# A vision tower on one core: constants and the first attention group loaded one stage ahead, attention output kept in 192 rows with its sums inverted early, row numbers copied by another engine

## The chip, the cores and the metric

The kernel runs on one core of a Trainium2 chip. A core has TensorE (PE, matrix multiplication into PSUM), VectorE (DVE), ScalarE (ACT), GpSimd (POOL) and SyncE (SP, which here only issues DMAs), one instruction stream each. They meet through semaphores. DMAs are issued by SP, ACT and POOL and carried by the core's 16 DMA engines. The metric is the device time of one launch in microseconds (us).

## The reference

The reference takes 8 images through a tower of two blocks, with 1030 tokens of 192 features per image:

```python
h = _L0_tok_ref(x, W0, b0, W1, b1, W2, b2)                 # patches of 8, 16, 32 pixels
h = concatenate([cls_tok, h], axis=1)
h = h + _L0_attn_ref(_layernorm(h), W_qkv, b_qkv)           # retention with a decay mask
h = h + _L0_ffn_ref(_layernorm(h), ...)                     # 16 experts pick their tokens, and a shared one
h = h + _L1_attn_ref(_layernorm(h), Wq, Wkv, Wo_ctx, ...)   # attention, below
h = h + _L1_ffn_ref(_layernorm(h), w_router, ...)           # 8 experts, 2 per token, and a shared one
```

The second block's attention has 12 heads of 16 features. The last 32 tokens ("latent") look at all 1030, the 998 before them only at each other, and each kind has its own output projection:

```python
kv = _heads(x @ Wkv);  q = _rope(q) * DH ** (-0.5);  kv = _rope(kv)
lkv = _ln(kv, ln_g, ln_b)
attn_lat = softmax(einsum('bid,bkd->bik', q_lat, kv))
attn_ctx = softmax(einsum('bid,bkd->bik', q_ctx, kv_ctx))
out_lat = _merge(attn_lat @ lkv) @ Wo_lat + bo_lat
out_ctx = _merge(attn_ctx @ lkv_ctx) @ Wo_ctx + bo_ctx
```

All is float32.

## The kernel before, in words

The work is a row of stages, each with its own block of instructions for every engine and a barrier at its end: patches, retention, route (with the first block's shared expert), experts, heads, attend, project, dispatch, mixture, output. Inside a block the order on each engine is the order of the code, written by hand with ring buffers and semaphore counts; there is no planner for it but in attend, where a written table gives the places of the latent steps. What a stage leaves for the next lies in DRAM (`h_rows`, `y_rows`, `qk_parts`, `o_parts`, `x_rows`), with a few exceptions.

*Constants.* Each stage has its own buffers for its constants and for an identity matrix `ident`. They are loaded at the start of the stage on SP's queue (in project on ACT's), and the stage's TensorE and DVE streams begin with a wait for all of them. In retention seven constants (L286) stand ahead of the first rows h_in (L289).

*heads* makes q, k and v of one image after another. For image b SP stores four parts of q and k (L1347, each waits for its part) and the values (L1350, L1352). The stage ends when the last image's stores have landed.

*attend* works on 24 groups of 4 heads, three to an image. A group needs 18 loads of q and k (L1697 to L1701) and two of v (L1705, L1707), in three buffers in turn. TensorE makes scores (L1772 for the maxima, L1846 for the exponentials), DVE reduces maxima (L1947), ACT takes exponentials (L1902), and TensorE multiplies by v (L1832). v has padding columns so that a head takes 32 rows of the result O [128 x 1030]: 16 features, one row with the sum of the exponentials, 15 unused. ACT copies O out of PSUM in two halves (L1892) when the group before is stored, DVE adds the latent columns (L1970), and POOL stores O with one DMA into `o_parts` (L1752).

*project* first loads all sums [96 x 1030] out of `o_parts`, inverts them on DVE (L2244) and stores them to `recips`. Then for each image SP loads op [128 x 3 x 1030] (L2082), the reciprocals spread over the rows (L2086, four DMAs) and the residual h_in (L2089). DVE scales (L2222), TensorE multiplies by Wo in 3 blocks of 128 rows for each of 9 token tiles and 2 kinds of job, 54 instructions to an image (L2140), DVE adds the residual (L2232) and takes the layer norm (L1242 to L1253), TensorE transposes (L2154) and makes the router's logits (L2162), and ACT stores.

*mixture* runs 72 chunks of 256 rows in a ring of 4. For each chunk POOL copies the row numbers to `idx` (L2693), runs a small addition `pad` (L2687), and gathers rows with two indirect DMAs (L2701); then it copies the numbers to `to` (L2707), again `pad`, and scatters the results with two indirect DMAs that add (L2715). Gathers are issued four chunks ahead. TensorE transposes the rows (L2745), makes the down projection of the chunk before (L2788) and gate and up of this one (L2763 to L2769). DVE multiplies the hidden values (hT), copies xT, and scales the results.

## Time and profile before

| | us |
|---|---|
| median of 3 runs (lowest, highest) | 4608.73 (4606.34, 4609.55) |
| the profiled execution's own time | 4602.88 |
| its span in the trace | 4601.2 |
| TensorE busy | 3963.6 (86%) |
| DVE busy | 2468.1 (54%) |
| ACT busy | 1440.2 (31%) |
| POOL busy | 1193.5 (26%) |
| mean granted clock of TensorE | 0.926 |

The first instructions behind each barrier stand at these times of the trace: retention 126.21, route 474.19, experts 890.55, heads 1807.85, attend 2124.69, project 3399.90, dispatch 3643.59, mixture 3975.27. POOL's set-up memsets are over at 131.8 in retention, 477.4 in route and 891.0 in experts. Busy shares are means over stages with different limits, so a stage's window and its timeline say more than these totals. POOL's busy time doesn't count the gaps in which it only issues.

### The profile page before, as it was taken

To read this page: it belongs to the slowest core of one execution; us is meant where nothing else is said; L and a number is where in the kernel's file an instruction comes from.
4 is the path that set the end of the run, shared out by engine and by line. 5 is a ranking of instruction groups with operands and counts; after the bars stand their busy time and mean duration, and the time that the engine had idled before them with its cause. 6 is when DMAs were issued, how large, how long until landed. Compare 5 with 4: busy or idle time off the path is not lost. (4 is left out here: it accounts for less than half of the span.)

```text
span 4601.2 us, 74362 instructions
## 1 busy us (share of the span) xinstructions
PE 3963.6 (86%) x24044; PEld 2468.0 (54%) x24046; DVE 2468.1 (54%) x4416; ACT 1440.2 (31%) x2890; POOL 1193.5 (26%) x1370
## 2 busy tenths in 40 slices
PE   8799787699999997665999999999958599898885
PEld 8688555466666665341333333333327466666664
DVE  1476368622222232886777777777714454444442
ACT  0122110011111111341777777777741111111110
POOL 0222000134444443553000000000013200277775
PEclk9899899899999998775999999999977699999998
DMA  6121111223222222345333233324139311377676
GB/s 211 48 66 52 38 41 35 66 51 66 63 59 59 59 60 62 111 138 107 51 63 48 48 61 57 47 48 66 34 91 249 92 32 52 93 163 160 157 161 149
DMA packets 335641, 381.02 MB, mean 83 GB/s; under 512 B 44708, under 2 KB 292035, under 8 KB 333823
## 3 DMA queue, kind: packets, MB, share of 16 engines
q1 hardware_dynamic: 255903, 289.44, 26.0%
q0 software_dynamic: 57856, 69.18, 8.9%
q10 hardware_dynamic: 21728, 20.14, 1.5%
q8 instruction: 122, 2.00, 0.2%
q14 instruction: 32, 0.26, 0.0%
HBM read 261.02 MB, written 123.33 MB: 84 GB/s over the span
## 5 line engine op out<-in xcount | busy, mean ns | idle before, releaser
L1947 DVE TENSOR_REDUCE at_mx<-psum 128x1 f32<-128x998 f32 (+1 forms) x768 | 886.6, 1193 | 261.2 <-PE psum L1772 260.8
L1902 ACT ACTIVATE at_p<-psum 128x512 f32<-128x512 f32 (+3 forms) x1536 | 851.7, 588 | 297.1 <-PE psum L1846 267.6
L1846 PE MATMUL psum<-at_q,at_k 99*128 99x512 bf16 (+3 forms) x1536 | 521.0, 382 | 20.9 <-issue 15.8
L1772 PE MATMUL psum<-at_k,at_q 96*128 96x512 bf16 (+3 forms) x1536 | 474.8, 392 | 67.0 <-DMA at_k<-qk_parts 29.6
L1832 PE MATMUL psum<-at_p,at_v 128*32 128x486 f32 (+3 forms) x3072 | 406.0, 601 | 1.0 <-ACT at_p L1902 0.7
L1846 PEld LDWEIGHTS psum<-at_q,at_k 99*128 99x128 bf16 (+1 forms) x1536 | 155.3, 102 | 424.9 <-ACT at_p L1902 268.0
L1158 ACT ACTIVATE ex_silu<-psum 128x384 f32<-128x384 f32 (+1 forms) x288 | 131.8, 458 | 773.0 <-PE psum L1102 643.2
L1189 DVE TENSOR_TENSOR ex_hT<-ex_silu,psum 128x384 f32<-128x384 f32 (+1 forms) x288 | 147.6, 513 | 415.4 <-ACT ex_silu L1158 270.4
L1752 POOL DMA_DIRECT2D o_parts<-at_o x24 | 13.0, 541 | 1245.3 <-DVE at_mx L1947 999.8
L1124 PE MATMUL psum<-ex_wd,ex_hT 128*128 128x192 f32 (+1 forms) x1728 | 291.5, 327 | 0.0
L1772 PEld LDWEIGHTS psum<-at_k,at_q 96*128 96x128 bf16 (+1 forms) x1536 | 152.2, 105 | 229.3 <-DVE at_mx L1947 64.0
L1124 PEld LDWEIGHTS psum<-ex_wd,ex_hT 128*128 128x128 f32 (+1 forms) x1728 | 264.1, 179 | 15.9 <-issue 3.6
L2826 ACT ACTIVATE mx_silu<-psum 128x256 f32<-128x256 f32 x216 | 83.0, 384 | 517.1 <-PE psum L2768 466.9
L2715 POOL DMA_INDIRECT h_rows<-mx_ys,mx_to x144 | 229.6, 1595 | 58.6 <-issue 58.4
L1050 POOL DMA_INDIRECT y_rows<-ex_ys,ex_to x144 | 223.3, 1550 | 33.4 <-issue 33.4
L1097 PE MATMUL psum<-ex_xT,ex_wg 128*128 128x384 f32 (+1 forms) x576 | 230.7, 482 | 0.0
L2855 DVE TENSOR_TENSOR mx_hT<-mx_silu,psum 128x256 f32<-128x256 f32 x216 | 91.1, 422 | 257.2 <-ACT mx_silu L2826 203.6
L1098 PE MATMUL psum<-ex_xT,ex_wu 128*128 128x384 f32 (+1 forms) x576 | 214.0, 453 | 0.0
L1102 PE MATMUL psum<-ex_xT,ex_wr 64*128 64x384 f32 (+1 forms) x576 | 204.8, 475 | 0.0
L1103 PE MATMUL psum<-ex_xT,ex_wr 64*128 64x384 f32 (+1 forms) x576 | 204.8, 475 | 0.0
L2701 POOL DMA_INDIRECT mx_xs<-x_rows,mx_idx x144 | 145.3, 1009 | 53.9 <-issue 50.8
L2788 PE MATMUL psum<-mx_wd,mx_hT 128*128 128x192 f32 x864 | 154.1, 329 | 0.8 <-DVE mx_ys L2865 0.8
(360 smaller groups left out, 6733.4 us busy)
## 6 DMA issues: line engine op xcount, KB each, us to landing
mx_wd<-in_e_dT SPq DMA_DIRECT2D x72, 288.0 KB
qk_parts<-hd_parts SPq DMA_DIRECT2D x32, 579.4 KB, 3.8
at_k<-qk_parts SPq DMA_DIRECT2D x144, 128.8 KB
at_q<-qk_parts SPq DMA_DIRECT2D x144, 124.8 KB
tok_p<-in_x SPq DMA_DIRECT2D x12, 1176.0 KB
mx_wg<-in_e_gT SPq DMA_DIRECT2D x72, 192.0 KB
mx_wu<-in_e_uT SPq DMA_DIRECT2D x72, 192.0 KB
o_parts<-at_o POOLq DMA_DIRECT2D x24, 515.0 KB
```

The lines of the kernel that those rows point to most:

```text
L1050: pool.indirect_dma_start(y, bass.IndirectOffsetOnAxis(ap=to[0:n, half, t:t + 1], axis=0), ys[0:n, half, t, :], None, compute_op=ALU.add). ...
L1097: g = pe.matmul(gate, wg[:, half, cols], xT[:, 0, toks], start=first, stop=not first)
L1098: u = pe.matmul(lift, wu[:, half, cols], xT[:, 0, toks], start=first, stop=not first)
L1102: g = pe.matmul(gate, wr[0:64, half, cols], xT[0:64, 1, toks], start=first, stop=not first)
L1103: u = pe.matmul(lift, wr[64:128, half, cols], xT[64:128, 1, toks], start=first, stop=not first)
L1124: mm = pe.matmul(psum[0:n, 4 + p % 2, (t % 2) * D:(t % 2 + 1) * D], hT[:, f, 128 * t:128 * t + n], wd[:, half, f, :], start=(f == 0), stop ...
L1772: mm = pe.matmul(psum[0:ctx_rows[t], 3 + 2 * ((PRO + n) % 2) + k, 0:w], Q[v][0:R6, j * 1024 + 128 * t:j * 1024 + 128 * t + ctx_rows[t]], K ...
L1832: mm = pe.matmul(psum[32 * j:32 * j + HV, 7, 0:w], V[u][0:n, t, j * HV:(j + 1) * HV], P[0:n, c % 2, j, 0:w], start=(t == 0), stop=(t == CT ...
L1846: pe.matmul(psum[0:n, i % RING, 0:w], K[u][:, j, 128 * t:128 * t + n], Q[u][:, j * 1024 + at:j * 1024 + at + w], start=True, stop=True).th ...
L1902: act.activation(P[0:n, c % 2, j, 0:w], psum[0:n, i % RING, 0:w], ACT.Exp).then_inc(exp_ready, 1)
L1947: dve.tensor_reduce(mx[0:ctx_rows[t], j * CT + t:j * CT + t + 1], pair(n)[0:ctx_rows[t], 0:CTX], AX_X, ALU.max).then_inc(s_free, 1)
L2715: pool.indirect_dma_start(y, bass.IndirectOffsetOnAxis(ap=to[:, r, t:t + 1], axis=0), ys[:, r, t, :], None, compute_op=ALU.add).then_inc(a ...
```

## The change

1. *Constants one stage ahead.* One `ident` is loaded in patches and kept. Retention's constants are loaded in patches (SP, behind the loads of the first two pairs), route's in retention (behind h_in), heads' in experts (behind the first two experts' weights), project's in attend (SP, behind the third group's loads), dispatch's in project (13 DMAs on ACT's queue at the start of the stage).
2. *Attend's first group* is loaded at the end of heads, on SP, ahead of the last image's stores.
3. *Attend's output* goes into `o_rows` [8 x 192 x 1030] without the unused rows: for each group four DMAs of 16 rows and four that bring a row of sums into a small buffer. DVE inverts them in the next group, and POOL stores them.
4. *project* no longer inverts sums. It loads 128 + 64 features per image, with 17 DMAs, and multiplies in two blocks instead of three, 36 instructions. ACT issues no constants of project.
5. *mixture*: the copies of the row numbers go from POOL to DVE.

The core of the diff:

```diff
-            for b in range(B - 3, B):
+            for b in range(B - 3, B - 1):
                 store(b)
+
+            for q in range(QC):
+                sp.wait_ge(parts_out[q], 16 * (B - 1))
+            load_quad(sp, qk_parts, 0, 0, first[0], first[1], loaded)
+            sp.wait_ge(v_stored, 32 * (B - 1))
+            load_quad_values(sp, v_rows, 0, 0, first[2], v_loaded)
+            store(B - 1)
...
-            load(0, 0)
             load(0, 1)
-            load_values(0, 0)
             load_values(0, 1)
             put_maxima(0, S_FREE0 + CT * QH + 3)
             load(0, 2)
             load_values(0, 2)
+            load_project_consts(sp, inp, project, project_in)
...
+            def store_shares(g):
+
+                pool.wait_ge(shares_ready, g + 2)
+                dst = recips[bass.ds(g, 1)].rearrange("a h (r c) -> (a h r) c", c=T)
+                pool.dma_start(dst, shares[:]).then_inc(shares_stored, 16)
+
+            def store(b, u, g, jobs, first=False):
                 pool.wait_ge(s_free, jobs)
                 pool.wait_ge(o_ready, 2 * g + 2)
-                dst = o_parts[bass.ds(b, 1), u].rearrange("b p n -> (b p) n")
-                pool.dma_start(dst, O[:]).then_inc(o_stored, 16)
+                pool.wait_ge(shares_ready, g + 1)
+                for j in range(QH):
+                    head = (u * QH + j) * DH
+                    dst = o_rows[bass.ds(b, 1), head:head + DH].rearrange("b d n -> (b d) n")
+                    pool.dma_start(dst, O[32 * j:32 * j + DH, :]).then_inc(o_stored, 16)
+                    row = O[32 * j + DH:32 * j + DH + 1, :].rearrange("a (r c) -> a r c", c=T)
+                    pool.dma_start(sums[NC * j:NC * (j + 1), :], row).then_inc(o_stored, 16)
+                if not first:
+                    store_shares(g - 1)
...
                 if h == 0:
-                    act.wait_ge(o_stored, g * 16)
+                    act.wait_ge(o_stored, g * STORE)
...
+            def shares_of(g):
+
+                dve.wait_ge(o_stored, g * STORE)
+                if not isinstance(g, int) or g:
+                    dve.wait_ge(shares_stored, (g - 1) * 16)
+                dve.reciprocal(shares[:], sums[:]).then_inc(shares_ready, 1)
...
                         dve.tensor_copy(O[:, CTX:SEQ], pair(n)[:, 0:LAT]).then_inc(s_free, 1)
+                        shares_of(g)
...
-            sp.dma_start(sums[:], o_parts.rearrange("b q (j r) n -> (b q j) r n", r=32)[:, DH, :]).then_inc(sums_in, 16)
-            sp.wait_ge(recip_ready, 1)
-            sp.dma_start(recips.rearrange("b h n -> (b h) n"), shares[:]).then_inc(recip_stored, 16)
-            sp.wait_ge(recip_stored, 16)
             sp.wait_ge(zeroed, ZEROED)
...
-                    sp.dma_start(op[:, half], o_parts[bass.ds(b, 1)].rearrange("a q p n -> p (a q) n")) \
-                        .then_inc(loaded[half], 16)
-                    for j in range(4):
-                        src = recips.rearrange("b (q j) n -> b j q n", j=4)[bass.ds(b, 1), j]
-                        sp.dma_start(recip[32 * j:32 * j + 32, half], src.broadcast_to([32, QUADS, SEQ])) \
-                            .then_inc(loaded[half], 16)
+                    src = o_rows[bass.ds(b, 1)].rearrange("a d n -> (a d) n")
+                    for f, (at, n) in enumerate(FEATS):
+                        sp.dma_start(op[0:n, half, f, :], src[at:at + n]).then_inc(loaded[half], 16)
+                    for h in range(HEADS):
+                        f, at = divmod(h * DH, 128)
+                        src = recips.rearrange("(b q) j n -> b (q j) n", b=B)[bass.ds(b, 1), h]
+                        sp.dma_start(recip[at:at + DH, half, f, :], src.broadcast_to([DH, SEQ])).then_inc(loaded[half], 16)
...
+            def rows_of(c, r, n_gathered):
+
+                if n_gathered is not None:
+                    dve.wait_ge(gathered[r], n_gathered)
+                here = ids[:, bass.ds(c * GS, GS)]
+                dve.tensor_tensor(idx[:, r, :], here, here, ALU.bitwise_or).then_inc(idx_ready, 1)
+
+            def rows_to(c, r):
+
+                if not isinstance(c, int) or c >= RING:
+                    dve.wait_ge(added, (c - RING + 1) * GATHER)
+                here = ids[:, bass.ds(c * GS, GS)]
+                dve.tensor_tensor(to[:, r, :], here, here, ALU.bitwise_or).then_inc(to_ready, 1)
...
                 hidden(c, i, r)
+                if ahead:
+                    rows_of(c + AHEAD, (r + AHEAD) % RING, None if first and r == 0 else (i + (r + AHEAD) // RING) * GATHER)
                 if following:
                     take_rows(c + 1, (r + 1) % RING, (i + (r + 1) // RING) * GATHER + GATHER)
+                rows_to(c, r)
```

Three places show what moves. The first is SP's queue at the end of heads and the start of attend. Before (hd_ is of heads, at_ of attend; `at_q0` is the first group's q):

```order
L1347 DMA qk_parts<-hd_parts 96x3x1030 x4
L1350 DMA v_rows<-hd_v_out 128x8x384
L1352 DMA v_rows<-hd_v_out 6x384
L1268 UNCONDITIONAL_BRANCH
L1687 UNCONDITIONAL_BRANCH
L1689 DMA at_ident<-in_ident 128x128
L1697 DMA at_q0<-qk_parts 16x4x998
```

After, with the end of the first group's loads:

```order
L1319 DMA at_k0<-qk_parts 16x4x1030
L1325 DMA at_v0<-v_rows 128x8x128
L1326 DMA at_v0<-v_rows 6x128
L1410 DMA qk_parts<-hd_parts 96x3x1030 x4
L1413 DMA v_rows<-hd_v_out 128x8x384
L1415 DMA v_rows<-hd_v_out 6x384
L1340 UNCONDITIONAL_BRANCH
L1769 UNCONDITIONAL_BRANCH
L1315 DMA at_q1<-qk_parts 16x4x998
```

The 20 loads of the first group have moved in front of the last image's stores, and the second group's loads now come first behind the branch into attend.

The second is POOL's stream in mixture, one chunk. Before:

```order
L2693 COPY mx_idx<-slot_rows 128x2
L2694 REGISTER_ALU
L2687 TENSOR_TENSOR mx_pad<-mx_ident 128x1
L2701 DMA mx_xs<-x3_rows,mx_idx 128x200 x2
L2707 COPY mx_to<-slot_rows 128x2
L2710 REGISTER_ALU
L2687 TENSOR_TENSOR mx_pad<-mx_ident 128x1
L2715 DMA h4_rows<-mx_ys,mx_to 8496x192 x2
```

After:

```order
L2765 TENSOR_TENSOR mx_pad<-ident 128x1
L2779 DMA mx_xs<-x3_rows,mx_idx 128x200 x2
L2785 REGISTER_ALU
L2787 REGISTER_ALU
L2792 REGISTER_ALU
L2765 TENSOR_TENSOR mx_pad<-ident 128x1
L2794 DMA h4_rows<-mx_ys,mx_to 8496x192 x2
```

Both copies are gone from POOL. The third is DVE's stream there, a chunk at the end of the stage. Before:

```order
L2855 TENSOR_TENSOR mx_hT<-mx_silu,psum 128x256 x3
L2834 TENSOR_TENSOR mx_hot_share<-mx_xs,chunk_hot 128x16
L2838 TENSOR_REDUCE mx_share<-mx_hot_share 128x2
L2843 COPY mx_xT<-psum 128x256
L2845 COPY mx_xT<-psum 64x256
L2846 COPY mx_xT<-psum 64x256
L2865 TENSOR_TENSOR mx_ys<-psum,mx_share 128x384
```

After:

```order
L2948 TENSOR_TENSOR mx_hT<-mx_silu,psum 128x256 x3
L2914 TENSOR_TENSOR mx_idx<-slot_rows 128x2
L2927 TENSOR_TENSOR mx_hot_share<-mx_xs,chunk_hot 128x16
L2931 TENSOR_REDUCE mx_share<-mx_hot_share 128x2
L2936 COPY mx_xT<-psum 128x256
L2938 COPY mx_xT<-psum 64x256
L2939 COPY mx_xT<-psum 64x256
L2921 TENSOR_TENSOR mx_to<-slot_rows 128x2
L2958 TENSOR_TENSOR mx_ys<-psum,mx_share 128x384
```

`mx_idx` is written between the hidden values and the copies of xT, `mx_to` between those copies and the results.

## Rows read from the trace of the kernel before

**Rows 1.** Windows, one per stage: busy us of each engine, clock, DMA share, GB/s.
```profile
890.00:1808.00 918.00, 884.31 (x4320) 603.58 (x4320) 260.91 (x528) 131.76 (x288) 392.30 (x450) 0.98 0.29 60
...
2125.00:3400.00 1275.00, 1188.74 (x9048) 399.26 (x9048) 947.92 (x984) 903.24 (x1705) 23.77 (x33) 0.96 0.32 51
3400.00:3643.00 243.00, 167.51 (x876) 150.89 (x876) 103.11 (x316) 36.24 (x88) 68.13 (x32) 0.70 0.73 188
...
3975.00:4569.00 594.00, 519.53 (x2880) 395.53 (x2880) 243.96 (x648) 82.98 (x216) 429.80 (x576) 0.98 0.70 156
```

**Rows 2.** Timeline, retention's start: SP's queue, DVE.
```profile
148.13 2.14 SPq L289 DMA_DIRECT2D ret_h_in<-h_rows  x4
...
154.17 1.14 DVE L507 BATCH_NORM_STATS2 ret_stats<-ret_h_in 103x6 f32<-103x192 f32 x4 [3.77 <-DMA ret_h_in<-h_rows]
```

**Rows 3.** Timeline, route's start: POOL, DVE.
```profile
476.83 0.52 POOL L683 MEMSET rt_zero<- 128x512 bf16 x1
...
486.22 0.77 DVE L829 COPY rt_gpad<-rt_gate 96x32 f32<-96x32 f32 x8 [11.83 <-DMA sh_wd<-in_sh_dT]
```

**Rows 4.** Timeline, heads' start: DVE, TensorE.
```profile
1821.09 2.67 DVE L1253 TENSOR_SCALAR hd_xn<-hd_rows,hd_mv,hd_rstd 128x192 f32<-128x192 f32 x9
...
1826.68 1.73 PE L1432 MATMUL psum<-hd_ident,hd_xn 128*96 128x128 f32 x7 [31.40 <-DMA hd_sin<-in_rope_sin]
```

**Rows 5.** Timeline, starts of experts (POOL) and dispatch (POOL, DVE).
```profile
892.44 0.19 POOL L1025 COPY ex_idx<-ids 128x9 int32<-128x9 int32 x1 [1.43 <-DMA ex_ident<-in_ident]
...
3645.13 0.57 POOL L2373 MEMSET di_slot<- 128x576 f32 x1
...
3655.22 0.23 DVE L2477 CAST di_iota_lo<-di_iotas 128x128 bf16<-128x128 f32 x1 [26.22 <-DMA di_wd<-in_s_dT]
```

**Rows 6.** Timeline and window, end of heads, start of attend: SP's queue, POOL, TensorE.
```profile
2104.70 10.29 SPq L1347 DMA_DIRECT2D qk_parts<-hd_parts  x4
...
2135.59 0.29 POOL L1746 CAST at_identb<-at_ident 128x128 bf16<-128x128 f32 x1
...
2140.70 1.82 PE L1772 MATMUL psum<-at_k,at_q 96*128 96x512 bf16 x4 [29.64 <-DMA at_k<-qk_parts]
...
2125.00:2150.00 25.00, 7.94 (x17) 1.26 (x18) 8.19 (x8) 0.00 (x0) 10.70 (x8) 0.50 1.04 121
```

**Rows 7.** Steady attend: timeline of POOL and ACT; dispatch's POOL DMAs by line.
```profile
3308.13 0.53 POOL L1752 DMA_DIRECT2D o_parts<-at_o  x1 [48.55 <-DVE at_mx L1947]
...
3330.91 0.58 ACT L1892 COPY at_o<-psum 128x512 f32<-128x512 f32 x1
...
L2381 POOL DMA_DIRECT2D x_rows<-di_expd x9: 601/886/1431, 3674.0 to 3681.6; - x9
```

**Rows 8.** Timeline, end of attend and start of project: POOL, DVE.
```profile
3393.64 0.53 POOL L1752 DMA_DIRECT2D o_parts<-at_o  x1 [38.71 <-ACT at_o L1892]
...
3403.42 6.59 DVE L2244 RECIPROCAL pr_shares<-pr_sums 96x1030 f32<-96x1030 f32 x1 [26.64 <-DMA pr_sums<-o_parts]
...
3436.68 3.38 DVE L2222 TENSOR_TENSOR pr_on<-pr_op,pr_recip 128x3090 f32<-128x3090 f32 x1 [1.72 <-DMA pr_hin<-y_rows]
```

**Rows 9.** Project's scalings by line, and two windows of the stage.
```profile
L2222 DVE TENSOR_TENSOR pr_on<-pr_op,pr_recip x8: 3351/3356/3379, 3436.7 to 3595.3; 128x3090 f32<-128x3090 f32 x8
...
3436.00:3455.00 19.00, 11.74 (x54) 10.94 (x54) 6.21 (x10) 0.00 (x0) 7.11 (x2) 0.75 1.06 262
...
3579.00:3596.00 17.00, 16.19 (x81) 15.10 (x80) 13.16 (x43) 2.42 (x6) 7.05 (x2) 0.71 0.35 102
```

**Rows 10.** Mixture: POOL's copies by line; timeline of POOL and TensorE.
```profile
L2693 POOL COPY mx_idx<-slot_rows x13: 751/761/771, 4198.4 to 4294.6; 128x2 int32 x13
...
4199.43 0.19 POOL L2687 TENSOR_TENSOR mx_pad<-mx_ident 128x1 f32<-128x1 f32 x1 [0.23 <-POOL mx_idx L2693]
...
4198.26 0.65 PE L2745 MATMUL psum<-mx_ident,mx_xs 128*128 128x128 f32 x4 [1.88 <-DMA mx_xs<-x_rows,mx_idx]
...
4205.28 0.66 PE L2745 MATMUL psum<-mx_ident,mx_xs 128*128 128x128 f32 x4
```

More of the change, by code:

```diff
@@ L2092, in _ @@
         def _(pool):
-            for buf in (wo[:], gain[:], shift[:], hin[:], mv[:], xn[:], logits):
+            for buf in (hin[:], mv[:], xn[:], logits):
                 pool.memset(buf, 0.0).then_inc(zeroed, 1)
@@ new lines, in build @@
+        project = project_consts(ctx, nc)
+        with ExitStack() as quads:
+            first = quad_buffers(quads, nc, 0)
+            with ExitStack() as middle:
+                heads = heads_consts(middle, nc)
+                phase_experts(nc, psum, inp, xg, y, ids, ident, ident_in, heads, heads_in)
+                phase_heads(nc, psum, inp, y, qk_parts, v_rows, ident, ident_in, heads, heads_in, first, loaded, v_loaded)
+            phase_attend(nc, psum, inp, qk_parts, v_rows, o_rows, recips, ident, ident_in, first, loaded, v_loaded,
+                         project, project_in)
@@ new lines, in build @@
+        slots = sb("slot_rows", [128, NSL], I32)[:]
+        chunk_expert, chunk_hot = sb("chunk_expert", [1, NCH], I32)[:], sb("chunk_hot", [128, NCH, E1])[:]
+        with ExitStack() as late:
+            dispatch = dispatch_consts(late, nc)
+            x3T = late.enter_context(nc.sbuf_tensor("x3T", [DP, DC, B, SEQ], F32))[:]
+            logits = late.enter_context(nc.sbuf_tensor("logits", [128, NTC * B, E1], F32))[:]
+            phase_project(nc, psum, inp, o_rows, recips, y, h3, x3T, logits, xg3, ident, ident_in, project, project_in,
+                          dispatch, dispatch_in)
+            phase_dispatch(nc, psum, inp, h3, x3T, logits, h4, xg3, slots, chunk_expert, chunk_hot, ident, ident_in,
+                           dispatch, dispatch_in)
@@ L2920, in build @@
+        phase_mixture(nc, psum, inp, xg3, h4, slots, chunk_expert, chunk_hot, ident, ident_in)
         phase_output(nc, h4, out)
```

428 lines of the change are left out of this document (219 added, 209 removed).

## The prediction

> **What bounds the kernel now.** I read the table of windows first, since the stages have different limits [rows 1]. In attend TensorE is busy 1188.7 of 1275 us at a clock of 0.96: that stage is TensorE's, and only its ends can be won. In project TensorE is busy 167.5 of 243 us at 0.70, DVE 103.1, and the DMA engines 0.73: three partners hand on to each other. In mixture TensorE is busy 519.5 and POOL 429.8 of 594 us; POOL's figure leaves out issue gaps, so the timeline has to decide there. Then I read the timeline of each stage's first microseconds [rows 2 to 5], because every stage ends in a barrier and whatever is loaded behind it stands on the path; then the boundary heads to attend [rows 6], one group of attend [rows 7], the start and period of project [rows 8, 9], and the loop of mixture [rows 10].
>
> **Constants, stage by stage.** *Retention* [rows 2]. The four h_in loads are issued at 148.13 because seven constants stand ahead of them on SP's queue; the first statistics follow at 154.17, 6.0 later. The barrier is over at 126.2 (the list of stage starts ahead), so after the change h_in is issued there and the statistics start at 132.3; POOL's memsets are over at 131.8 and don't hold them: −21.9. The constants, some 0.8 MB, go behind the patches' first two pairs' loads and wait for nobody there. *Route* [rows 3]. DVE waits until 486.22 for sh_wd; POOL's last memset ends at 477.4. −8.8. *Experts* [rows 5]. POOL's first copy waits for ident until 892.44, its memset was done at 891.0: −1.4. *Heads* [rows 4]. The xn of the first tile is written from 1821.09, TensorE starts at 1826.68, held by sin. With the constants there it starts about 1.3 behind 1821.09: −4.3. *Dispatch* [rows 5]. DVE waits until 3655.22 for di_wd. The logits are there and POOL's last memset ends at 3645.7, so DVE starts there: −9.4. *Mixture* starts like experts: −1.4. Together −47.2. Each stands on a row that names a constant's landing as the last releaser; what is late next is named above (memsets, h_in). Bounds −40 to −50. If the covers were gone (heads' 3.75 MB go beside experts, DMA share 0.29 [rows 1]), each would pay its own row again, at most.
>
> **Heads to attend.** SP's order changes (the first of the three places shown with the change). Before, SP stores the last image part by part from 2104.70, the stage ends at 2124.7, attend's first group is issued behind that, and TensorE starts at 2140.70 [rows 6]. After, 20 loads of the first group (about 1.5 MB of q and k, 0.5 MB of v) stand ahead of the last image's stores, and the 18 of q and k wait until the image before has landed. Attend's start: POOL's cast of identb, behind its memsets, ends at 2135.88, 11.2 behind the barrier, so TensorE can start at +11.5 rather than at +16: −4.5. Heads' end: 2 MB at the 121 GB/s of the row is 16 us, the queue is empty in part, and the four parts become ready one after another over 10.3 us (the length of the row at 2104.70), which covers part of it; I take +7.5 (bounds 0 and +12). Net +3, from −4.5 to +7.5. This is the one edit I expect to lose.
>
> **Attend.** One POOL DMA of 0.53 us per group becomes nine. In the steady state POOL stores O at 3308.13, and ACT writes it again at 3330.91 [rows 7]: 22.8 us. A POOL DMA cost 0.53 here and 0.89 in dispatch, so the eight are issued in 4.3 to 7.1 us, and with 3.3 to land they are done in 7.6 to 10.4. Hidden. DVE gets one reciprocal of 103 elements a row per group: by the 6.59 us for 1030 [rows 8] 0.7 us, on an engine busy 948 of 1275 us [rows 1]. For that I take +2, bounds 0 and +8. The Trainium skill (DMA: Bandwidth & Descriptors, section Anatomy of one DMA) speaks against the split: each DMA of this path costs some 2.0 us whatever its size, plus its bytes over 436 GB/s, and its section Bandwidth asks for 1 MiB per transfer. By that, eight one behind the other (66 KB and 4 KB in turn) would take an estimated 16.6 us, still inside the window, but 9 us more at the end of attend: a sum of −135 instead of −144. No row here shows eight in a row.
>
> **Project's start.** Before: the last POOL store at 3393.64, the reciprocal 96x1030 of 6.59 us at 3403.42, first scaling at 3436.68 [rows 8], 43.0 us from the store. After: eight POOL DMAs (+4.6), landing 3.3 (in either kernel a guess from the block's end 6.3 behind the store), the small reciprocal 0.8, the store of the shares with its landing 4.0: attend ends near 3406.5 instead of 3399.9. Then op, recip and hin of image 0, 2.4 MB, need 10 to 13 us at 180 to 260 GB/s and 15 issues some 8 us: scaled at 3424 to 3427. Dispatch's constants, 1.1 MB, now run on ACT's queue at the same moment: +3 (4 us at 262 GB/s, part of it beside POOL's memsets). So 3429.7 instead of 3436.7: −7 (bounds −13 and 0).
>
> **Project's period.** The eight scalings run from 3436.7 to 3595.3, 22.7 us apart [rows 9]. The DMA engines are at 1.06 in the first of them and at 0.35 in the last stretch, so they bound the stage most of the time, not always. Bytes per image: op and recip 2 x 1.58 MB, hin 0.79, two stores of 0.79: 5.5 MB. After: 2 x 0.79 + 0.79 + 1.58 = 3.95 MB, 0.71 of it: 16.2 us. TensorE's work of one image is 81 instructions of 16.2 us at a clock of 0.71 (the last stretch); 18 of its 54 products of 0.22 go: 12.3, and with the hand-overs some 14.8. DVE loses 2 x 128x1030 in part, 3.36 us to about 2.2. I take 16.5, above both: 7 x 6.2 = −43, and −3 for the last image: −46. Bounds: −20 (SP needs 17 issues per image instead of 8, and waits on stores stay) and −60.
>
> **Mixture.** POOL's copies start 8.01 us apart (13 starts, 4198.4 to 4294.6), and POOL waits for nothing but itself [rows 10]. The order shows two COPY rows less per chunk. The copy in front of the gather overlaps the DMA ahead of it but for some 0.2, and the pad behind it waits 0.23 for it (the row at 4199.43); the copy in front of the scatter, 0.2 long, the same: 0.86 together, POOL's round goes to 7.15. TensorE waits 1.88 us for the gather at 4198.26, and its one unblocked round is 4198.26 to 4205.28, 7.02. Into its chain goes rows_of, which DVE now does between hT and the copies of xT that TensorE needs: about 0.2, so 7.2. Two rounds so close collide now and then: I take 7.3. (8.01 − 7.3) x 69 = −49. Bounds: −59 (7.15) and −15 (7.8, if rows_of and rows_to both add their wait, some 0.3 each, to TensorE's chain and the gather comes later by it).
>
> **Sum.** −47.2 +3 +2 −7 −46 −49 = −144. The profiled execution's own time was 4602.9 (span 4601.2, 1.7 around it); that gives 4459. It lay 5.9 under the median of the runs shown, 4608.7, so I forecast 4464.5.
>
> **Rivals.**
> (1) *Mixture keeps its time.* DVE's rows become the bound: TensorE's chain 7.02 + 0.6 and the hand-over give 7.8. For: no slack was seen between DVE's last copy of xT and TensorE. Against: DVE is busy 244 of 594 us. Time 4464.5 + 34 = 4498.
> (2) *Project isn't bound by bytes.* The small DMAs, 17 per image, take SP's queue 12 us and more, and the store to load waits stay: 20 us per image, −20. For: the share falls to 0.35 at the end without a shorter period. Time 4464.5 + 26 = 4490. With (1), 4524.
> (3) *The boundaries cost more*: heads ends 12 later instead of 7.5 and attend's first groups are late, or POOL's eight DMAs at the end of attend go one behind the other: in series, each with the 3.3 until it has landed, they take 26 us; for the end alone +9 to +18: 4474 to 4483.
> (4) *More than forecast*: mixture at 7.15, project at 15: 4464.5 − 10 − 14 = 4440.
> (5) *Slower.* Attend's DMAs don't fit the window: ACT's copy at 3330.91 stalls, and behind it the exponentials that TensorE waits for. It costs from (22.8 − 3.3)/8 = 2.4 us per DMA on, and 23 groups pay. For no gain they would need 6.3 us more per group, 3.2 us per DMA; for slower by 0.2% 3.3 us and above: 4618 and more. Against: 0.53 and 0.89 in the rows, 1.43 the longest. In series at 3.3 each the eight would overrun the window by 3.6 us, 23 times: +83, 4547, still faster.
> (6) *The change doesn't do what it says*: constants hidden before already. The releasers in rows 2 to 5 exclude it for the constants; if project and mixture both gave nothing, 4560.
>
> **How the numbers follow.** Chances: forecast (4448 to 4480) 0.46, (1) 0.15, (2) 0.13, both 0.05, (3) 0.06, (4) 0.08, (5) 0.03, (6) 0.04. What a measurement tells from no change is 0.2%, about 9 us. Slower is (5), 0.03, and same a partial (5) or (6), 0.02: faster 0.95. The range takes in (1) to (4): from 4425 (both large terms at their favourable bound, −59 and −57) to 4520 (short of (1) and (2) together), and leaves 0.2 outside.
>
> **What would show it.** In the profile after: the first statistics of retention near 132; TensorE's start of attend 11.5 us behind its barrier, and heads longer by 7; in attend no wait of ACT for a DMA at the copy of O; scalings 16 to 17 us apart in project; POOL's pads ahead of the gather 7.2 to 7.4 apart in mixture, with no copy on POOL. I would be wrong by a lot if TensorE's clock changed: it stood at 0.70 in project, and at a lower share of the full clock its chain of 14.8 becomes the bound; or if DVE's waits for landed scatters, which it didn't have before, came on TensorE's path.

## The result and the profile after

The changed kernel takes 4569.3 us (median of 4 runs, 4568.0 to 4576.5), the kernel before 4609.1 on the same chip: ratio 0.9916 [0.9903, 0.9929]. That is 40 us faster where I forecast 144, and outside my range of 4425 to 4520. The profiled execution took 4569.56 us, its span 33.4 less than that of before.

The page of the kernel after: span, busy times, and the clock in 40 slices.

```profile
span 4567.8 us, 74772 instructions
...
PE 4034.8 (88%) x23898; PEld 2458.2 (54%) x23898; DVE 2484.5 (54%) x4593; ACT 1438.0 (31%) x2890; POOL 1249.9 (27%) x1415
...
PEclk9999988899999998775999999999975589999998
```

TensorE has fewer instructions in project than before, and yet 71 us more busy time over the whole kernel. In the second group of low digits of PEclk, three quarters of the way along, stand two fives: that is project. Split by stage, from POOL's first instruction behind each barrier to the next one's, and mixture from its first gather to its last scatter (us):

| | before | after | change | forecast |
|---|---|---|---|---|
| patches | 126.2 | 130.8 | +4.6 | 0 |
| retention | 348.0 | 328.4 | −19.6 | −21.9 |
| route | 416.4 | 415.7 | −0.7 | −8.8 |
| experts | 917.3 | 918.3 | +1.0 | −1.4 |
| heads | 316.8 | 323.9 | +7.1 | +3.2 |
| attend | 1275.2 | 1278.0 | +2.8 | +4.1 |
| project | 243.7 | 262.4 | +18.7 | −59.6 |
| dispatch, mixture's start | 334.1 | 324.0 | −10.1 | −10.8 |
| mixture's chunks | 591.1 | 553.8 | −37.3 | −49 |
| sum | 4568.8 | 4535.3 | −33.5 | −144.2 |

Project alone misses by 78 of the 111 us. Here are its windows after (columns as in [rows 1]), its TensorE timeline over one image, and the waits of DVE (us in total, times, longest).

```profile
3440.00:3480.00 40.00, 37.67 (x111) 23.69 (x112) 19.54 (x75) 6.06 (x13) 11.07 (x5) 0.50 0.58 167
3480.00:3520.00 40.00, 38.16 (x137) 23.74 (x137) 17.27 (x57) 6.91 (x17) 7.84 (x5) 0.59 0.49 131
```

```profile
3441.56 16.52 PE L2246 MATMUL psum<-pr_wo_g,pr_on 128*128 128x192 f32 x36 [2.81 <-DVE pr_on L2320]
3458.00 2.29 PE L2260 MATMUL psum<-ident,pr_xn 128*96 128x128 f32 x9
3460.61 2.22 PE L2260 MATMUL psum<-ident,pr_xn 128*96 128x128 f32 x9 [0.31 <-ACT pr_xT L2303]
3463.30 7.15 PE L2268 MATMUL psum<-pr_router,pr_xT 96*128 96x8 f32 x36 [0.47 <-ACT pr_xT L2303]
3470.37 4.76 PE L2246 MATMUL psum<-pr_wo_g,pr_on 128*128 128x192 f32 x10
```

```profile
DVE pr_hout L2331 <- PE psum L2246: 56.1, 26, 3.9
...
DVE pr_hout L2331 <- DMA h_rows<-pr_hout: 7.9, 4, 3.9
```

The 36 products of an image take 16.5 us; 54 took 10.5 to 12.0 before (11.74 in the first window of [rows 9], at a clock of 0.75). TensorE goes from one piece of work to the next with gaps of 0.3 to 0.5 us: busy 38 of 40 us, at 0.50, the lower of its two levels (1.2 of 2.4 GHz). The DMA share has gone down to 0.58 and 0.49. Nobody waits long for a store any more (7.9 us in all, where before DVE waited 31.1 and 27.7 us for the stores of `pr_hout` and `pr_xn`); DVE waits for TensorE. So the bytes did shrink as forecast, and TensorE became the bound with a period of 26 to 29 us (the first products of the images from the second on start at 3441.6, 3470.4, 3496.9, 3524.4, 3553.2, 3579.9 and 3606.4).

Mixture: TensorE's transposes of two chunks (timeline), POOL's pads, DVE's new row, and a window.

```profile
4204.84 0.66 PE L2824 MATMUL psum<-ident,mx_xs 128*128 128x128 f32 x4
...
4212.36 0.66 PE L2824 MATMUL psum<-ident,mx_xs 128*128 128x128 f32 x4
```

```profile
4212.14 0.75 POOL L2765 TENSOR_TENSOR mx_pad<-ident 128x1 f32<-128x1 f32 x1
...
4215.99 0.19 POOL L2765 TENSOR_TENSOR mx_pad<-ident 128x1 f32<-128x1 f32 x1 [0.65 <-DVE mx_ys L2958]
```

```profile
4205.70 0.15 DVE L2914 TENSOR_TENSOR mx_idx<-slot_rows 128x2 int32 x1
```

```profile
4200.00:4300.00 100.00, 97.99 (x538) 72.79 (x538) 47.57 (x147) 15.68 (x41) 75.25 (x81) 1.00 0.72 172
```

The same window of before had TensorE busy 90.4 us. Now it is busy 98 of 100, and POOL waits at times for DVE's results (0.65 us at 4215.99): the bound has passed from POOL to TensorE, at 7.5 us a round.

The starts of the stages, timeline rows after: SP and DVE in retention, DVE in route, TensorE in heads, DVE in dispatch.

```profile
130.75 1.85 SPq L319 DMA_DIRECT2D ret_h_in<-h_rows  x4
...
136.78 2.17 DVE L539 BATCH_NORM_STATS2 ret_stats<-ret_h_in 103x6 f32<-103x192 f32 x8 [0.20 <-DMA ret_h_in<-h_rows]
...
462.36 0.78 DVE L846 COPY rt_gpad<-rt_gate 96x32 f32<-96x32 f32 x8 [3.00 <-POOL rt_zero L699]
...
1807.59 2.32 PE L1502 MATMUL psum<-ident,hd_xn 128*96 128x128 f32 x9 [26.82 <-DVE hd_xn L1288]
...
3659.74 0.23 DVE L2557 CAST di_iota_lo<-di_iotas 128x128 bf16<-128x128 f32 x1 [17.34 <-POOL di_slot L2452]
```

No constant is a releaser any more: the engines wait for h_in, for POOL's memsets and for xn, as each row of [rows 2 to 5] was expected to end. In route DVE starts 3.2 us behind the barrier at 459.2 (before 12.0), and the stage still takes as long. A window of route after, with the clock in the third column from the end:

```profile
685.00:725.00 40.00, 31.31 (x339) 22.58 (x338) 31.91 (x25) 2.05 (x4) 0.00 (x0) 0.80 0.12 32
```

Its counterpart before, from 700:

```profile
700.00:740.00 40.00, 31.31 (x366) 22.35 (x358) 34.67 (x28) 3.08 (x6) 0.00 (x0) 0.94 0.13 33
```

The end of heads and start of attend, and steady attend (ACT's copy is the one that overwrites the O that POOL has stored):

```profile
2094.59 7.07 SPq L1410 DMA_DIRECT2D qk_parts<-hd_parts  x4
...
2128.26 0.29 POOL L1815 CAST at_identb<-ident 128x128 bf16<-128x128 f32 x1
...
2128.61 1.85 PE L1858 MATMUL psum<-at_k,at_q 96*128 96x512 bf16 x4 [31.92 <-POOL at_identb L1815]
...
3292.60 0.50 POOL L1830 DMA_DIRECT2D o_rows<-at_o  x1 [44.19 <-DVE at_mx L2033]
...
3296.61 0.55 POOL L1821 DMA_DIRECT2D recips<-at_shares  x1
...
3315.39 0.58 ACT L1978 COPY at_o<-psum 128x512 f32<-128x512 f32 x1
```

And the end of attend, POOL and DVE:

```profile
3378.13 0.50 POOL L1830 DMA_DIRECT2D o_rows<-at_o  x1 [34.68 <-ACT at_o L1978]
...
3381.63 0.52 POOL L1832 DMA_DIRECT2D at_sums<-at_o  x1
...
3383.89 0.79 DVE L2053 RECIPROCAL at_shares<-at_sums 40x103 f32<-40x103 f32 x1 [21.92 <-DMA recips<-at_shares]
...
3384.97 0.52 POOL L1821 DMA_DIRECT2D recips<-at_shares  x1 [2.28 <-DVE at_shares L2053]
...
3395.11 2.98 POOL L2199 MEMSET pr_hin<- 128x3456 f32 x1 [9.62 <-POOLq L62]
```

### The profile page after: what moved, and what is told of

It reads as the page before. It is cut to its first block and busy times, and to the rows that moved or that the text cites. A ratio compares the mean times of both kernels' runs of the same rounds, so it can differ in the third digit from the quotient of the medians.

```text
span 4567.8 us, 74772 instructions
## 1 busy us (share of the span) xinstructions
PE 4034.8 (88%) x23898; PEld 2458.2 (54%) x23898; DVE 2484.5 (54%) x4593; ACT 1438.0 (31%) x2890; POOL 1249.9 (27%) x1415
## 5 line engine op out<-in xcount | busy, mean ns | idle before, releaser
L1932 PE MATMUL psum<-at_q,at_k 99*128 99x512 bf16 (+3 forms) x1536 | 518.9, 380 | 21.5 <-issue 16.5
L1830 POOL DMA_DIRECT2D o_rows<-at_o x96 | 48.5, 505 | 1140.3 <-DVE at_mx L2033 967.0
L1085 POOL DMA_INDIRECT y_rows<-ex_ys,ex_to x144 | 223.4, 1551 | 33.5 <-issue 33.5
L2765 POOL TENSOR_TENSOR mx_pad<-ident 128x1 f32<-128x1 f32 x144 | 66.1, 459 | 353.6 <-DVE mx_idx L2914 301.9
L1050 POOL TENSOR_TENSOR ex_pad<-ident 128x1 f32<-128x1 f32 x127 | 41.5, 327 | 438.0 <-DVE ex_ys L1237 430.9
```

The costliest lines, as they stand in the source:

```text
L1085: pool.indirect_dma_start(y, bass.IndirectOffsetOnAxis(ap=to[0:n, half, t:t + 1], axis=0), ys[0:n, half, t, :], None, compute_op=ALU.add). ...
L1932: pe.matmul(psum[0:n, i % RING, 0:w], K[u][:, j, 128 * t:128 * t + n], Q[u][:, j * 1024 + at:j * 1024 + at + w], start=True, stop=True).th ...
```

## The experiments

On project there were four theories. **S**: each change between a product over 128 rows and one over 64 costs TensorE a fixed time, and these gaps keep the clock low. **M**: products over 64 rows are another form of work, which by itself keeps the clock low. **F**: what counts for the clock is how many of the 128 rows the products use, at first told as the mean over all of them. **W**: not TensorE but waits, for stores or for the 17 loads, set the period. For the other differences: **a**, retention's constants lengthen patches; **C**, what an earlier start wins is given back by the clock; **D**, POOL has to drain its many small DMAs at the end of attend. All kernels compute everything; p128 and p80 multiply rows of zeros besides. Ratios are to the kernel before on the same chip; its median was 4607.0 to 4616.4 on the chips used.

**p96**: the 192 features as 96 + 96, with as many instructions as the changed kernel.

```diff
-    FEATS = ((0, 128), (128, D - 128))
+    FEATS = ((0, 96), (96, 96))
...
-                        f, at = divmod(h * DH, 128)
+                        f, at = divmod(h * DH, 96)
```

 Then without the switch the 36 take 6 to 9 us per image, scalings come 15 to 18 us apart, and the stage falls from 262 to about 165 to 185 us: 4475 to 4495 in all. Theory F (fill): the clock stays low since on average only 96 of 128 rows are used. That is the same here: 36 x 0.38 = 13.7 instead of 16.5, the clock stays at 0.50, about -25 us: 4545. Theory W (waits for stores and loads bound the stage): no change, 4569.

Measured: 4480.8 us (4473.2 to 4491.8), ratio 0.972 [0.970, 0.974]. Project takes 184.4 us, 78 less than after. Window and TensorE's products:

```profile
3440.00:3480.00 40.00, 38.14 (x210) 34.32 (x210) 26.72 (x98) 8.84 (x22) 11.65 (x6) 0.80 0.88 235
```

```profile
3452.97 9.55 PE L2246 MATMUL psum<-pr_wo_g,pr_on 96*128 96x192 f32 x36
...
3469.96 9.58 PE L2246 MATMUL psum<-pr_wo_g,pr_on 96*128 96x192 f32 x36
```

The same number of instructions takes 9.6 instead of 16.5 us, and the period is 17.0. SP still issues 17 loads per image: W falls. F falls too in its first form: the products use 96 rows on the mean here as in the changed kernel, and by F the clock would have stayed at 0.50 and the time at 4545.

**p128**: 128 + 64 as in the changed kernel, but the second product runs over all 128 rows, of which 64 hold zeros.

```diff
-                            mm = pe.matmul(psum[...], on[0:r, f, at:at + n],
-                                           wo_g[0:r, int(t == 8), f, :], ...)
+                            mm = pe.matmul(psum[...], on[:, f, at:at + n],
+                                           wo_g[:, int(t == 8), f, :], ...)
```

> The changed kernel with the second block of project's products run over 128 rows, 64 of them zeros (two more memsets on POOL). Theory S: as 96 + 96, 15 to 18 us per image, 4477 to 4497 (1.5 us more at the stage's start). Theory F: all 128 rows are used, so the clock rises as before and the time falls as well, to the same figure; F and S differ in the 96 + 96 kernel. Theory W: no change, 4569.

Measured: 4489.5 us (4486.1 to 4500.9), ratio 0.975 [0.973, 0.977]; project 187.9.

```profile
3440.00:3480.00 40.00, 34.01 (x196) 30.08 (x193) 29.27 (x85) 10.72 (x27) 12.64 (x6) 0.79 0.91 239
```

```profile
3448.05 8.52 PE L2246 MATMUL psum<-pr_wo_g,pr_on 128*128 128x192 f32 x36
```

This is the change's own split, and multiplying zeros makes project 74.5 us shorter. The 64 rows of data aren't what costs; the 64-row form of the instruction is, by S, M or F.

**p64**: three blocks of 64 features, 54 instructions, none of them of another height.

```diff
-    FEATS = ((0, 128), (128, D - 128))
+    FEATS = ((0, 64), (64, 64), (128, 64))
```

> The changed kernel with project's contraction cut 64 + 64 + 64: 54 instructions per image as before the change, all of 64 rows, no switch. Theory S: TensorE runs them like the 54 of before, 11 to 12 us per image, and the clock rises as often as before (mean 0.7); the stage takes about 185 to 200 us. Theory F: only half of the rows is ever used, the clock stays at 0.50, 54 x 0.38 = 20.4 us per image and some 36 us apart: the stage takes about 320 us. Theory W: 262 as in the changed kernel.

Measured (one run): 4582.6 us; project 278.1.

```profile
3480.00:3520.00 40.00, 39.22 (x141) 35.45 (x140) 15.41 (x53) 4.48 (x11) 5.83 (x3) 0.50 0.67 171
```

```profile
3474.20 17.78 PE L2246 MATMUL psum<-pr_wo_g,pr_on 64*128 64x192 f32 x54
```

Without any change of height between products the clock stays at 0.50 to 0.54, so S isn't the whole of it. No theory had this time: S said 185 to 200 for the stage, F 320, W 262. The row also gives the price of one instruction at that clock: 17.78/54 = 0.33 us. By it the 36 of the changed kernel should take 11.9; they take 16.5. The trace shows two instructions for each product of the code, one behind the other (that, and not two kinds of job as the description of the kernel before has it, is why 9 tiles x 2 blocks give 36), so 17 changes of height lie among them: (16.5 − 11.9)/17 = 0.27 us each. The weight loads of the changed kernel show the same change by change:

```profile
3471.31 0.50 PEld L2246 LDWEIGHTS psum<-pr_wo_g,pr_on 64*128 64x128 f32 x2 [0.44 <-issue]
3472.25 0.50 PEld L2246 LDWEIGHTS psum<-pr_wo_g,pr_on 128*128 128x128 f32 x2 [0.44 <-issue]
```

Two instructions and one change take 0.94 us. Where the height stays, in p64, instructions start 0.32 us apart, 0.64 for two. So a change costs 0.30 us at this clock.

**snake**: the changed kernel with the order of the two blocks turned round in every second tile (128, 64, 64, 128, ...), which leaves about half of the changes.

```diff
-                        for f, (_, r) in enumerate(FEATS):
+                        for m in range(2):
+                            f = (m + t) % 2
```

> The changed kernel with the order of the two blocks turned round in every second token tile (128, 64, 64, 128, 128, ...), so that there are half as many switches between row counts. Theory S: half of the extra time per instruction goes (0.46 to 0.42 at the low clock, 15.1 instead of 16.5 us per image), and if the clock rises in some stretches, more: the stage falls by 10 to 60 us. Theory F: the fill is the same, the clock stays at 0.50; only the part of the switch itself can go, -11 us. Theory W: no change.

Measured (one run): 4549.2 us; project 247.1, 15.3 less than after.

```profile
3461.41 14.49 PE L2248 MATMUL psum<-pr_wo_g,pr_on 128*128 128x192 f32 x36
```

14.49 − 11.85 = 2.6 us for the 9 changes that are left: 0.29 us each. S holds for the price. The clock was 0.54 to 0.55 in its windows: fewer changes didn't bring it up.

**p80**: as p64, but each product runs over 80 rows, 16 of them zeros, so that no product is over 64 rows any more.

```diff
-                            mm = pe.matmul(psum[...], on[0:r, f, at:at + n],
-                                           wo_g[0:r, ...], start=(f == 0), stop=(f == 1))
+                            mm = pe.matmul(psum[...], on[0:80, f, at:at + n],
+                                           wo_g[0:80, ...], start=(f == 0), stop=(f == 2))
```

> The 64 + 64 + 64 kernel with 16 rows of zeros added to each block, so that the 54 products per image run over 80 rows instead of 64. In the 64-row kernel there is no switch between row counts, and yet the clock stayed at 0.50 to 0.54. Theory M (products of 64 rows or fewer are another form of work, which by itself keeps the clock low): with 80 rows the clock is at 0.7 to 0.8 again, and 54 products take 11 to 13 us per image: the stage takes 190 to 215 us. Theory F (the share of rows in use sets it): 80 of 128 is 0.63, below the 0.75 of 96 rows: the clock stays at 0.54 and the stage takes 270 to 285.

Measured (one run): 4596.8 us; project 278.2, as p64.

```profile
3480.00:3520.00 40.00, 38.62 (x162) 35.16 (x161) 16.49 (x62) 7.58 (x19) 11.65 (x6) 0.57 0.42 116
```

```profile
3459.14 17.78 PE L2246 MATMUL psum<-pr_wo_g,pr_on 80*128 80x192 f32 x54 [3.95 <-DVE pr_on L2320]
```

80 rows behave like 64, to the hundredth of a microsecond: M falls. (The total is 14 us above p64's because experts, whose code is the same, took 934.8 us for 917.1.) F's figure for this run came true, but what is left of F is only that a stage of such products, all below 96 rows, ran at the low clock here. In the three windows from 3440 to 3560 the clock was 0.50 to 0.57 with products over 64 or 80 rows alone, 0.50 to 0.59 with 128 and 64 in turn, and 0.71 to 0.80 with 96 or 128 (before, p96, p128), though TensorE was the busier in the low ones: 35 to 39 of 40 us, against 31 to 38. That is the observation. A rule by rows alone doesn't follow from it: the changed kernel and p96 use the same 96 rows on the mean, one at 0.50 to 0.59 and one at 0.76 to 0.80, and mixture has products over 64 rows at a clock of 1.00, in pairs that start within 0.01 us of each other. The runs show that changes of height and low products each came with the low clock in this stage; what sets it stays open.

**mix**: the kernel before with the mixture edit alone (row numbers copied by DVE).

```diff
-                pool.tensor_copy(idx[:, r, :], ids[:, bass.ds(c * GS, GS)]).then_inc(idx_ready, 1)
...
+                dve.tensor_tensor(idx[:, r, :], here, here, ALU.bitwise_or).then_inc(idx_ready, 1)
```

> The kernel before with the edit of mixture alone (row numbers copied by DVE, pads with their own counts). Theory: the whole of mixture's gain is this edit, 591 to 553 us from the first gather to the last scatter, -37: 4571, ratio 0.992. Rival: part of it comes from ident being there or from the stage's start (1.4), or the edit does less without the rest: -30 or less, 4579.

Measured: 4572.2 us (4570.8 to 4572.5), ratio 0.993 [0.991, 0.995]. Its chunks take 553.4 us, as in the changed kernel (553.8) and 37.7 less than before; TensorE is busy 97.98 us in the window from 4200 to 4300. Mixture's gain comes from that edit alone. So small an edit makes nearly the gain of the whole change, since project eats the rest.

**nogroup** and **early_late**, both on p96. In nogroup attend loads its first group itself, as before the change. In early_late that group is loaded ahead of the stores of the last three images instead of the last one, and retention's constants behind all loads of patches.

```diff
             for q in range(QC):
-                sp.wait_ge(parts_out[q], 16 * (B - 1))
+                sp.wait_ge(parts_out[q], 16 * (B - 3))
...
-            store(B - 1)
+            for b in range(B - 3, B):
+                store(b)
```

> The 96 + 96 kernel with attend's first group loaded in attend again, as before the change. Theory (the boundary loses as forecast): heads 317 to 318 instead of 324.5, attend longer by 4.5 as TensorE starts 16 instead of 11.4 us behind the barrier: 2 us in favour of this kernel. Rival: heads stay at 324, since what makes them longer is not the order of the stores: then this kernel is 4.5 us slower.

> The 96 + 96 kernel with two moves. (a) Retention's constants go behind the last pair's loads in patches instead of between the second and the third pair's. Theory: the changed kernel's patches took 130.8 instead of 126.2 because the constants share the DMA engines with the first pair's weights; then patches take 126.2 again (the 96 + 96 kernel showed 127.2). Rival: the constants, now issued near 75, land so late that retention waits: retention longer by some us. (b) Attend's first group is loaded ahead of the stores of image 5 instead of ahead of those of image 7. Theory: the stage's end lay 20.4 us behind TensorE's last work instead of 13.6 because the last image's stores stood behind the 20 loads; then heads take 317 to 318 instead of 324.5, and attend keeps its start. Rival: the loads only delay another image's stores: heads stay at 324. Sum -8 against the 96 + 96 kernel, about 4472, ratio to before 0.970.

Measured: nogroup 4486.6 us (one run), early_late 4482.5 (4468.9 to 4488.7), ratio 0.974 [0.972, 0.976]. Heads and attend together take 1592.1 in the kernel before, 1601.9 after, 1608.4 in p96, 1605.9 in nogroup and 1585.0 in early_late: as the change has it, the early group gives nothing clear (the end of heads pays what the start of attend wins), and further ahead these stages were 21 us shorter than in nogroup. The two kernels below that keep it take 1595.5 (sptail) and 1587.6 (rtback2), of which 8 us may be owed to another edit; so it is worth between 2 and 21 us by single profiles. Much of that may be scatter: the seven kernels that load the first group as the change has it took 1600.2 to 1608.4 together. In the total early_late can't be told from p96, and it missed the 4472 expected. Patches is 127.3 in early_late, 127.2 in p96, 125.8 to 128.4 in all kernels but the changed one; a falls, and the 4.6 us of patches after are one profiled execution's.

**rtback**: p96 with route's constants loaded in route again.

```diff
-            load_route_consts(sp, inp, route, route_in)
...
+            load_route_consts(sp, inp, consts, consts_in)
```

> The 96 + 96 kernel with route's constants loaded at route's start again. In the changed kernel TensorE started 8.9 us earlier in route, but the stage took 415.7 instead of 416.4; three rounds between 675 and 730 took 3.2 us longer each, at a clock of 0.80 instead of 0.94. Theory C (the gain is lost to TensorE's clock, and with the constants back the clock rises where it rose before): the stage takes 416 to 417, as with the constants early. Rival (the early start is worth its 8.9 us, and the three slow rounds come from elsewhere in this kernel): the stage takes 425 to 428.

Measured (one run): 4501.1 us; route 422.4 against 418.8 in p96.

**sptail**: early_late's first group, and the last group's stores and reciprocals issued by SP instead of POOL.

```diff
+            for j in range(QH):
+                head = (2 * QH + j) * DH
+                sp.dma_start(o_rows[B - 1, head:head + DH], O[32 * j:32 * j + DH, :]).then_inc(o_last, 16)
...
-            for u in range(3):
+            for u in range(2):
```

> The 96 + 96 kernel with attend's first group loaded ahead of the stores of image 5 (that part took heads and attend from 1608 to 1585 together in the run before), and with the last group's eight stores and the last reciprocals issued by SP instead of POOL. In the changed kernel POOL stands 7.5 us in a drain at the end of attend, although its last DMA has landed; before the change, with one DMA at the end, 2.0. Theory D (the drain grows with the DMAs that POOL issued last): with none of them on POOL near the end it is 0 to 2 us, and attend ends 5 to 8 us earlier: attend 1264 to 1267 us where the run without this edit had 1271, total about 4467, ratio to before 0.969. Rival (the wait at the end is the landing of the stores, whoever issued them): SP's landings take as long, attend as before, 4475.

Measured: 4492.0 us (4474.8 to 4494.9), ratio 0.9714 [0.9693, 0.9735]. The end of attend, SP's last store and POOL's first row of project:

```profile
3396.24 0.30 SPq L1810 DMA_DIRECT2D recips<-at_shares  x1
...
3398.56 2.98 POOL L2213 MEMSET pr_hin<- 128x3456 f32 x1 [24.27 <-POOLq L62]
```

From ACT's last copy of O to project's first instruction it took 10.0 us (3388.52 to 3398.56); after, it took 18.1 (3377.00 to 3395.11), as in p96, and before 7.4. In the changed kernel everything had landed by some 3386.6, and POOL then stood in the drain at the end of its block for 7.5 us (3386.84 on; before 2.0). In sptail POOL issues one DMA near the end, 1.8 us before its drain, instead of ten, and its last batch of eight was issued 20 us earlier. The drain is still 6.75 long, but it is over before SP is. So D is wrong in its form (without the batch the drain was expected at 0 to 2) and right in its place: the way from the last copy to project is 8.1 us shorter. The stage as a whole doesn't show it: attend took 1278.8, against 1264 to 1267 expected and 1271.0 in early_late, and the total of 4492.0 is no better than early_late's.

**rtback2**: sptail with route's constants loaded in route, as rtback.

```diff
-            load_route_consts(sp, inp, route, route_in)
...
+            load_route_consts(sp, inp, consts, consts_in)
```

> The kernel with SP's tail, with route's constants loaded at route's start again: a second sample of that question with another history of TensorE's clock ahead of it. Theory C (the earlier start is lost to the clock): route takes as long as with the constants early, 412 to 419. Rival (it is worth 6 to 9 us): 421 to 427, as the first sample's 422.4.

Measured (one run): 4489.3 us; route 422.2, against 419.0 in sptail. Over all kernels route takes 412.5 to 419.3 with its constants ahead (9 kernels, mean 416.2), and 416.4, 416.4, 422.4 and 422.2 without (mean 419.4): some 3 us of the 8.8, and the two sets overlap. C's forecasts for the two (416 to 417, 412 to 419) both failed, and the rival's 421 to 427 held in rtback2; the kernels with 96 + 96 alone have 422.4 and 422.2 without against 412.5 to 419.0 with, some 6 us, while the kernel before and mix, without, took 416.4.

No version beat p96, early_late and sptail, whose ratios (0.972, 0.974, 0.9714) can't be told apart.

## Why the prediction was wrong, point by point

**Project's period is the step that failed**, and in it this sentence: "18 of its 54 products of 0.22 go: 12.3, and with the hand-overs some 14.8". It took the price of an instruction from rows in which all had 128 rows and the clock was 0.7 to 0.8, and assumed both for products of 64 rows. Measured, TensorE's work of one image is 28.2 us (16.5 + 2.3 + 2.2 + 7.2, the first four rows of its timeline above) instead of 12.3.

The 12.3 was too low already at the old price. The window that it starts from, "81 instructions of 16.2 us" [rows 9], is not one image: an image has 54 instructions for the products, 18 for the transposes and 36 for the router, 108 in all. Before, they take 10.94 + 1.08 + 1.47 + 0.32 + 4.70 = 18.5 us:

```profile
3458.88 10.94 PE L2140 MATMUL psum<-pr_wo_g,pr_on 128*128 128x192 f32 x54 [6.97 <-DVE pr_on L2222]
3469.75 1.08 PE L2154 MATMUL psum<-pr_ident,pr_xn 128*96 128x128 f32 x8
3471.15 1.47 PE L2154 MATMUL psum<-pr_ident,pr_xn 128*96 128x128 f32 x9 [0.32 <-ACT pr_xT L2206]
3472.86 0.32 PE L2154 MATMUL psum<-pr_ident,pr_xn 128*96 128x128 f32 x1 [0.25 <-ACT pr_xT L2206]
3473.46 4.70 PE L2162 MATMUL psum<-pr_router,pr_xT 96*128 96x8 f32 x36 [0.28 <-ACT pr_xT L2206]
```

Less 18 x 0.22 that is 14.5, and with the same 2.5 for hand-overs 17.0: above the 16.5 of the bytes, so TensorE was the bound even without a lower clock.

I had named a change of TensorE's clock as what would make me wrong by a lot, and gave it no chance. Against p96 the changed kernel loses 78 us: 17 changes x 0.30 x 8 images are 41 of them, and the other 37 I put down to the clock, by difference. The bytes did shrink, and the time forecast from them is met where products keep their height: 243.7 − 59.6 = 184.1 forecast, 184.4 in p96, with a period of 17.0 against my 16.5. But that is in part luck. TensorE is busy 38 of 40 us there beside a DMA share of 0.88, and its work of an image (9.6 + 1.1 + 1.5 + 0.3 + 3.9) is 16.3 of the 17.0 us, so TensorE sets the period there too, at the 17.0 of the sum just made; and project took 179.8 to 186.0 us over the six kernels with 96 + 96.

On the change of height the Trainium skill (TensorEngine Tiling (Array Packing), section Key Properties) says that changing the tiling mode drains TensorE. The trace agrees, with 0.30 us each at the low clock; I hadn't weighed it, and it was the rule that spoke against this change. The kernel before could have given the price. Mixture changes between 128 and 64 rows four times a round, at a clock of 1.00 (its products over 64 rows start in pairs):

```profile
4201.66 0.48 PE L2768 MATMUL psum<-mx_xT,mx_wr 64*128 64x256 f32 x1
4201.67 0.48 PE L2769 MATMUL psum<-mx_xT,mx_wr 64*128 64x256 f32 x1
4201.98 0.38 PE L2768 MATMUL psum<-mx_xT,mx_wr 64*128 64x256 f32 x1
```

The first pair behind the change holds TensorE for 0.32 us, later pairs for 0.21; the last product ahead of the change loses 0.09 as well: 0.20 us per change at the full clock.

**Mixture**: the mechanism was right, the size off. TensorE is the bound, as I had it; a round takes 7.45 on the mean (TensorE's transposes of the first and the last chunk start at 3987.21 and 4516.32, 71 rounds) where I took 7.3, and took 7.98 before, where I read 8.01 off thirteen starts. 0.18 us x 70 are the 12 us that are missing. `rows_of` is 0.15 long and stands where the order showed it. Rival (1), with 7.8, didn't come.

**Constants.** Retention −19.6 for −21.9: h_in is issued at 130.75, right behind the barrier at 130.8, and the statistics follow 6.0 later, as forecast. Dispatch −10.1 for −10.8. Heads: TensorE starts 14.4 behind the barrier instead of 18.8, −4.4 for −4.3; but the first 36 products behind it take 14.7 us where they took 12.0, at a window clock of 0.67 for 0.84, and TensorE's last work, counted from its first, is 4.7 later than before. Route: the start came 8.9 earlier and the gain was still there at 680 us; then three rounds lost about 3 us each, at a clock of 0.80 for 0.94. Both fit C, an engine that starts earlier and meets the low clock, but no run shows the cause, and in rtback and rtback2 C's forecast failed: route's constants are worth 3 to 6 us by the figures above, and the same code of route or experts varies by 6 and 20 us from kernel to kernel (412.5 to 419.3, 914.0 to 934.8). What grants or withholds the clock there stays open.

**Heads to attend**: attend's TensorE starts 11.5 behind the barrier, at identb, exactly as forecast (−4.5). The end of heads is 20.4 behind TensorE's last work instead of 13.6: +6.8 for +7.5. The net of +3 was right, and so was the sign: the one edit I expected to lose.

**Attend and its end**: the eight DMAs are issued in 4.0 us (the last at 3296.10 behind 3292.60, 0.52 long) and ACT overwrites O at 3315.39 without a wait, so rival (5) had no ground. At the end, DVE's reciprocal starts at 3383.89, 2.3 us behind the issue of the eighth DMA and 5.8 behind the first: the eight land side by side. The estimate of 16.6 us for eight in a row took the Trainium skill's 2.0 us per DMA (DMA: Bandwidth & Descriptors, section Anatomy of one DMA) eight times over. This trace doesn't bear out that sum: 5.8 us. What I left out was the drain, 7.5 us for 2.0: the end cost +10.7 against +6.6. The first scaling still comes 39.6 us behind the last copy of O instead of 44.2: −4.6 for −7.

**The other rivals.** Rival (2) gave the right direction for project, for another reason: it had SP's queue and the stores as the bound at 20 us, and its time of 4490 was still 79 short. Of the case that came, both a lower clock and a price for the changes, I had neither. The lower end of my range, 4425, doesn't follow from the bounds that I named for it: −59 for −49 and −57 for −46 give 4443.

## What to carry to other kernels

When matmuls are reshaped, don't price the new ones from rows of the old shape: look at how many rows each uses and at what height stands before it, and ask what the stage costs at TensorE's lower level. Equal heights (96 + 96) or a block padded with zeros to full height may be far cheaper than the split with the fewest rows. And when the work of a DMA-bound stage is cut, compute the period again with every other engine's worst price, since one of them will be the bound; and take an engine's work from all instructions of one image, not from a window as long as the period.

## What the runs showed of the hardware

- 54 instructions of products over 64 or over 80 rows took the same 17.78 us per image, at a clock of 0.50 to 0.57; 36 over 96 or 128 rows took 7.9 to 9.6 at 0.76 to 0.80 (p96, p128). In p128 and p80 the added rows held zeros.
- Products over 64 rows don't by themselves mean a low clock: mixture runs them in pairs, with four changes of height a round, at 1.00.
- One change between products over 128 and over 64 rows took 0.30 us at the low clock (project) and 0.20 us at the full clock (mixture).
- Eight small DMAs (66 and 4 KB in turn) from POOL's queue were issued 0.50 to 0.52 us apart and had all landed 5.8 us behind the first issue.
- POOL's drain at the end of attend was 7.5 us in all nine kernels with nine DMAs per group, 6.75 in sptail and rtback2 (one DMA in the last 20 us), 2.0 in the two with one DMA per group. In the other stages it was between 1.0 and 5.9, the same in all kernels; in heads 4.3, though POOL's last DMA lay over 300 us back. What it waits for is open.
- Stages whose code is the same differ by up to 20 us from one kernel to another (experts 914.0 to 934.8), and the profiles don't say why; gains of a few us at a boundary can't be verified in the total.
